# A normalised Gram matrix in the setup of a deformable-convolution kernel: norms applied to the images before, to the 64x64 products after

## What is computed

```python
x_flat = x.reshape(B, C, H * W)
nrm = jnp.linalg.norm(x_flat, axis=2, keepdims=True)
x_n = x_flat / jnp.maximum(nrm, 1e-12)
cos = jnp.einsum('bcn,bdn->cd', x_n, x_n) / B
_, idx = jax.lax.top_k(-jnp.abs(cos).T, k)          # k = 2
s = x.sum(axis=(2, 3)); sq = (x * x).sum(axis=(2, 3))
gs = s + s[:, idx[:, 1:]].sum(axis=-1)              # sums of the pair
...
x_hat = (x - mean[:, :, None, None]) * inv[:, :, None, None]
```

## Time and profile before

| | |
|---|---|
| median of 3 runs | 427.45 us (426.53 to 428.62) |
| the profiled execution, its own time | 429.34 us |
| its span, first to last instruction | 427.5 us |
| TensorE busy | 398.2 us, 93% |
| ScalarE busy | 327.0 us, 76% |
| VectorE busy | 312.3 us, 73% |
| GpSimd busy | 111.4 us, 26% |
| copy to `neg_cos` starts | 22.61 us |
| TensorE starts on the first layer | 27.97 us |

### The profile page before, as it was taken

The page is one execution under the profiler, slowest core; times in us unless marked ns, Lnnn a source line. Parts: engine busy times, 40 slices in busy tenths (PEclk is TensorE's granted clock), DMA queues, the critical chain, the costliest instruction groups (busy, mean ns, idle before and its releaser), DMA issues.

```text
span 427.5 us, 19117 instructions
## 1 busy us (share of the span) xinstructions
PE 398.2 (93%) x7747; PEld 357.9 (84%) x7747; DVE 312.3 (73%) x868; ACT 327.0 (76%) x423; POOL 111.4 (26%) x241
## 2 busy tenths in 40 slices
PE   4978899999999999999998899999999998999980
PEld 4865689999999999999885788999999997998870
DVE  3649877788887777777438888877777776777445
ACT  2617788888888898888835878888888887888745
POOL 6303223222222222238001322232222222220000
PEclk9999999999999999999999999999999999999996
DMA  6301342211122222222001231222222222222005
GB/s 220 84 2 34 71 69 48 45 36 36 38 46 46 44 44 46 49 48 41 2 3 28 57 62 38 50 45 46 45 45 45 48 48 47 48 48 40 3 2 196
DMA packets 61529, 21.28 MB, mean 50 GB/s; under 512 B 53798, under 2 KB 61308, under 8 KB 61484
## 3 DMA queue, kind: packets, MB, share of 16 engines
q1 hardware_dynamic: 56588, 18.20, 20.3%
q0 software_dynamic: 4896, 2.43, 2.2%
HBM read 3.23 MB, written 2.10 MB: 12 GB/s over the span
## 4 chain that ended last, share of the span: by engine, by line
PE 85%; DVE 5%; DMA 4%; ACT 2%; issue 2%; SPq 1%; POOL 1%; DVEq 0%; ACTq 0%; POOLq 0%
PE acc_ps L746 54%; PE z_ps L719 12%; PE build_ps L704 8%; PE side_ps L652 3%; PE acc_ps L770 3%; PE side_ps L641 2%; DMA xs<-in_x 2%; PE build_ps L588 1%; DMA moved<-conv_sb 1%; PE acc_ps L598 1%; DMA feat_rows<-feats 1%; ACT raw L563 1%; PE acc_ps L630 1%; SPq L278 1%; ACT S L482 0%
## 5 line engine op out<-in xcount | busy, mean ns | idle before, releaser
L746 PE MATMUL acc_ps<-S,Z 64*64 64x256 f32 x4416 | 279.4, 377 | 1.6 <-issue 0.9
L746 PEld LDWEIGHTS acc_ps<-S,Z 64*64 64x64 f32 x4416 | 225.3, 133 | 19.8 <-issue 3.5
L482 ACT ACTIVATE S<-build_ps,minus 128x1024 f32<-128x1024 f32 x190 | 201.5, 1112 | 30.6 <-PE build_ps L704 30.2
L719 PE MATMUL z_ps<-wz,xflat 64*64 64x192 f32 x1536 | 106.9, 328 | 0.0
L704 PE MATMUL build_ps<-feat_rows,cst 64*64 64x512 f16 x576 | 82.9, 377 | 3.3 <-ACT S L482 1.6
L475 ACT ACTIVATE Z<-z_ps 128x768 f32<-128x768 f32 x96 | 78.2, 814 | 4.9 <-PE z_ps L719 4.9
L719 PEld LDWEIGHTS z_ps<-wz,xflat 64*64 64x64 f32 x1536 | 75.8, 132 | 6.5 <-issue 1.3
L1007 DVE TENSOR_SCALAR S<-build_ps 128x512 f32<-128x512 f32 x96 | 66.1, 688 | 19.1 <-PE build_ps L704 17.3
L278 POOL DMA_DIRECT2D moved<-conv_sb x140 | 71.0, 514 | 20.6 <-POOL conv_sb L371 15.5
L1009 DVE TENSOR_SCALAR S<-build_ps 128x512 f32<-128x512 f32 x96 | 65.3, 680 | 0.0
L371 POOL TENSOR_TENSOR conv_sb<-conv_sb,cst 128x32 f32<-128x32 f32 x28 | 7.5, 269 | 200.5 <-ACT conv_sb L469 200.5
(11 more groups left out here) (116 smaller groups left out, 307.4 us busy)
## 6 DMA issues: line engine op xcount, KB each, us to landing
xs<-in_x SPq DMA_DIRECT2D x4, 512.0 KB, 7.5
out<-raw SPq DMA_DIRECT2D x7, 256.0 KB, 2.5
moved<-conv_sb POOLq DMA_DIRECT2D x56, 11.2 KB
moved<-conv_sb SPq DMA_DIRECT2D x56, 11.2 KB
moved<-conv_sb POOLq DMA_DIRECT2D x56, 11.3 KB
wz<-in_dcn_w POOLq DMA_DIRECT2D x2, 288.0 KB, 4.7
feat_rows<-feats SPq DMA_TRANSPOSE x32, 3.7
moved<-conv_sb SPq DMA_DIRECT2D x28, 12.0 KB
```

Of the source, the lines that this page charges most:

```text
L482: act.activation(S[:, (parity + b) % 2, half, 0:ACT_TAPS, :], build_ps[:, 0:ACT_TAPS, :], ACT.Relu, bias=minus2[:, :], scale=1.0 if half = ...
L719: mm = pe.matmul(z_ps[halves[c], i, h * BLOCK_COLS:(h + 1) * BLOCK_COLS], xflat[parity][halves[i], pixels], wz[halves[i], layer, h, b * BL ...
L746: mm = pe.matmul(acc_ps[halves[i], g, 0:HW], Z[halves[g], slot, i, half, j * C:(j + 1) * C], S[halves[g], slot, half, j, :].rearrange(by_i ...
```

## The change

TensorE now turns the images as they were loaded, and each image's 64x64 Gram product is kept for itself. The norms come in afterwards: an entry (c, d) of an image's product is multiplied by the reciprocal norm of row c and that of column d. The row's is `rinv` as before, a number for each partition. The columns' is made on TensorE: a product of `rinv`, spread over 64 columns, with the identity over 32 (`spread_rinv`) puts each image's reciprocals in every row of a 64x64 tile in `z_ps`. VectorE multiplies all three (`scale_dots`), from a copy of the products that ScalarE makes (`keep_gram`). Then 16 products with `fold` sum the images and the two halves at once (`fold_dots`), in the place of the scaling and the one product before.

The work goes by chunks: TensorE's order is turn(g), spread_rinv(g-1), gram(g), fold_dots(g-1). The ten fill products ahead are gone; two stand behind gram(0). `fold` is no longer loaded but made on GpSimd from the identity, as is `ident_by_count`. The scalings of the images are gone, L870 and L430. Nothing behind the copy to `neg_cos` is changed.

```diff
-        xn = raw
-        xn_t = S[:, 0, 0, :, :]
+        x_t = [S[:, 0, j // 2, j % 2, :] for j in range(4)]
+        dots = raw[:, :, 0:C]
+        kept_gram = raw[:, :, C:2 * C]
...
+        turn_banks = ((build_ps[:, 0, :], build_ps[:, 1, :]), (build_ps[:, 2, :], z_ps[:, 0, :]))
...
+            pool.wait_ge(ident_in, 16)
+            pool.wait_ge(cleared, 8)
+            for rows in halves:
+                pool.tensor_scalar(ident_by_count[rows, :], ident[rows, rows], 1.0 / B, None, ALU.mult).then_inc(folds_made, 1)
+            pool.wait_ge(folds_made, 2)
+            for rows in halves:
+                pool.tensor_copy(fold[rows, :].rearrange("p (c n) -> p c n", c=2),
+                                 ident[rows, rows].unsqueeze(1).broadcast_to([C, 2, C])).then_inc(folds_made, 1)
...
+                act.wait_ge(x_turned, j + 1)
+                if j >= 4:
+                    act.wait_ge(gram_done, j // 2 - 1)
+                act.activation(x_t[j % 4], turn_banks[j // 2 % 2][j % 2], ACT.Copy).then_inc(x_t_ready, 1)
+
+            def keep_gram(g):
+                act.wait_ge(gram_done, g + 1)
+                act.activation(kept_gram[:, g * CHUNK_PAIRS:(g + 1) * CHUNK_PAIRS, :],
+                               acc_ps[:, g % 2, 0:CHUNK_PAIRS * C].rearrange("p (t c) -> p t c", c=C), ACT.Copy).then_inc(gram_kept, 1)
...
-            norm(0)
-            for g in range(X_CHUNKS - 1):
-                act.wait_ge(rinv_step, 2 * (g + 1))
-                for t in (g * CHUNK_PAIRS + 2, g * CHUNK_PAIRS + 3):
-                    act.activation(xn[:, t, :], xs[:, t, :], ACT.Copy, scale=rinv[:, t:t + 1]).then_inc(xn_by_act, 1)
-                norm(g + 1)
+            for g in range(X_CHUNKS):
                 copy_turned(2 * g)
                 copy_turned(2 * g + 1)
-            copy_turned(PAIRS // 2 - 2)
-            copy_turned(PAIRS // 2 - 1)
+                norm(g)
+                keep_gram(g)
...
-            keep_busy(10)
...
+            def turn(g):
+                pe.wait_ge(x_in[g], 16)
+                if g >= 2:
+                    pe.wait_ge(x_t_ready, 2 * (g - 1))
+                for j in range(2):
+                    for i in range(2):
+                        for h in range(HALVES):
+                            q = 2 * i + h
+                            mm = pe.transpose(turn_banks[g % 2][j][:, q * P:(q + 1) * P],
+                                              xs[:, CHUNK_PAIRS * g + 2 * j + i, h * P:(h + 1) * P], ident)
+                    mm.then_inc(x_turned, 1)
+
+            def gram(g):
+
+                if g >= 2:
+                    pe.wait_ge(gram_kept, g - 1)
+                for n in range(CHUNK_PAIRS):
+                    if n % 2 == 0:
+                        pe.wait_ge(x_t_ready, 2 * g + n // 2 + 1)
+                    for h in range(HALVES):
+                        for i in range(2):
+                            at = (n % 2 * HALVES + h) * P + i * C
+                            slab = x_t[(2 * g + n // 2) % 4][:, at:at + C]
+                            mm = pe.matmul(acc_ps[halves[i], g % 2, n * C:(n + 1) * C], slab, slab,
+                                           start=(h == 0), stop=(h == HALVES - 1))
+                mm.then_inc(gram_done, 1)
+
+            def spread_rinv(g):
+
+                pe.wait_ge(rinv_step, 2 * (g + 1))
+                if g == 0:
+                    pe.wait_ge(folds_made, 4)
                 else:
+                    pe.wait_ge(scaled_dots, CHUNK_PAIRS * g)
+                for n in range(CHUNK_PAIRS):
+                    t = CHUNK_PAIRS * g + n
                     for i in range(2):
+                        mm = pe.matmul(z_ps[halves[i], 1, n * C:(n + 1) * C], rinv[halves[i], t:t + 1].broadcast_to([C, C]),
+                                       ident_by_count[halves[i], :], start=True, stop=True)
+                mm.then_inc(rinv_rows, 1)
+
+            def fold_dots(g):
+                for n in range(CHUNK_PAIRS):
+                    t = CHUNK_PAIRS * g + n
+                    pe.wait_ge(scaled_dots, t + 1)
+                    mm = pe.matmul(side_ps[:, 0, 0:C], fold[:, :], dots[:, t, :], start=(t == 0), stop=(t == PAIRS - 1))
+                return mm
 
             turn(0)
-            for j in range(1, PAIRS // 2):
-                turn(j)
-                gram(j - 1)
-            gram(PAIRS // 2 - 1)
-            pe.wait_ge(setup_dve, 1)
-            pe.wait_ge(consts_in, 16)
-            pe.matmul(side_ps[:, 0, 0:C], fold, gram_sb[:, :], start=True, stop=True).then_inc(gram_step, 1)
+            gram(0)
+            keep_busy(2, side_ps[:, 1, 0:P])
+            for g in range(1, X_CHUNKS):
+                turn(g)
+                spread_rinv(g - 1)
+                gram(g)
+                fold_dots(g - 1)
+            spread_rinv(X_CHUNKS - 1)
+            fold_dots(X_CHUNKS - 1).then_inc(gram_step, 1)
...
+            def scale_dots(g, n):
+
+                t = CHUNK_PAIRS * g + n
+                if n == 0:
+                    dve.wait_ge(rinv_step, 2 * (g + 1))
+                    dve.wait_ge(gram_kept, g + 1)
+                    dve.wait_ge(rinv_rows, g + 1)
+                dve.scalar_tensor_tensor(out=dots[:, t, :], in0=kept_gram[:, t, :], scalar=rinv[:, t:t + 1],
+                                         in1=z_ps[:, 1, n * C:(n + 1) * C], op0=ALU.mult, op1=ALU.mult).then_inc(scaled_dots, 1)
...
-            dve.wait_ge(gram_step, PAIRS // 2)
-            dve.tensor_scalar(gram_sb[:, :], acc_ps[:, 0, 0:C], 1.0 / B, None, ALU.mult).then_inc(setup_dve, 1)
```

More of the change, by code:

```diff
@@ L569, in _, with keep_busy @@
             pe.wait_ge(ident_in, 16)
-            def keep_busy(count):
+            def keep_busy(count, into=build_ps[:, BLOCK_TAPS - 1, 0:P]):
                 for n in range(count):
-                    pe.matmul(build_ps[:, BLOCK_TAPS - 1, 0:P], ident, ident, start=True, stop=True, skip_group_check=True)
-            keep_busy(10)
-            def turn(j):
-                if j == PAIRS // 2 - 1:
-                    pe.wait_ge(xn_by_dve, 2 * (X_CHUNKS + 1))
-                else:
-                    pe.wait_ge(xn_by_act if j % 2 else xn_by_dve, 2 * (j // 2 + 1))
-                if j >= 2:
-                    pe.wait_ge(xn_t_ready, j - 1)
-                for i in range(2):
-                    for h in range(HALVES):
-                        q = 2 * i + h
-                        mm = pe.transpose(build_ps[:, j % 2, q * P:(q + 1) * P],
-                                          xn[:, 2 * j + i, h * P:(h + 1) * P], ident)
-                mm.then_inc(xn_turned, 1)
@@ L592, in gram @@
-            def gram(j):
-                pe.wait_ge(xn_t_ready, j + 1)
-                for q in range(4):
-                    for i in range(2):
-                        at = q * P + i * C
-                        slab = xn_t[:, j % 2, at:at + C]
-                        mm = pe.matmul(acc_ps[i * C:(i + 1) * C, 0, 0:C], slab, slab, start=(j == 0 and q == 0),
-                                       stop=(j == PAIRS // 2 - 1 and q == 3))
-                mm.then_inc(gram_step, 1)
-            turn(0)
@@ L603, in _ @@
-            for j in range(1, PAIRS // 2):
-                turn(j)
-                gram(j - 1)
-            gram(PAIRS // 2 - 1)
-            pe.wait_ge(setup_dve, 1)
-            pe.wait_ge(consts_in, 16)
-            pe.matmul(side_ps[:, 0, 0:C], fold, gram_sb[:, :], start=True, stop=True).then_inc(gram_step, 1)
+                    pe.matmul(into, ident, ident, start=True, stop=True, skip_group_check=True)
+            def turn(g):
[9 more added lines that the diff above has]
+                    mm.then_inc(x_turned, 1)
@@ L847, in _ @@
                 pe.wait_ge(bn_dve, BN_OPS * layer + 1)
-                pe.matmul(side_ps[:, 1, 0:2], fold, bmv[:, :], start=True, stop=True).then_inc(bn_folded, 1)
+                pe.matmul(side_ps[:, 1, 0:2], fold[:, :], bmv[:, :], start=True, stop=True).then_inc(bn_folded, 1)
                 if layer == 0:
@@ L1126, in shape_constants @@
     put("ident", np.eye(P))
-    put("fold", part[:, None] % C == part[None, :] % C)
     taps = np.arange(TAPS).reshape(BLOCKS, BLOCK_TAPS, 1)
```

76 lines of the change are left out of this document (40 added, 36 removed).

## The result

The changed kernel takes 432.49 us (median of 6 runs, 430.88 to 433.48), the kernel before 427.73 in its 6 runs: a ratio of 1.0112, 95% interval 1.0091 to 1.0133. Slower by 4.8 us, where 0.3 less was forecast.

A forecast was written before the change was run, and what follows sets the result against it. TensorE was taken to bound the setup, the layers staying unchanged. The steps put the neg_cos copy at 22.3 instead of 22.6 us, so -0.3 us and a median of 427.1, range 425.0 to 429.3 us.

The forecast's parts named there:

- The diff changes no instruction of that stretch: The two deformable layers, 28 to 415 us: 387 us long and unchanged, so only their start could move.
- a layer stretch that is not 387 us long: Sign of a wrong forecast: the two deformable layers, expected as long as before, take another time.
- nobody waits for: Setup: the ten fill products from 4.73 us in the kernel before, taken as work no engine needs.
- the start 5.8 us earlier: Setup: TensorE's real work begins at 4.73 instead of 10.51 us, no longer waiting for normalised images.
- -0.3: Forecast change in us: neg_cos copied at 22.3 instead of 22.6, everything behind it equal.
- Step 4 of the chain: Setup's end: last reciprocal rows to 21.1, four scalings to 21.8, last fold to 22.3, where neg_cos is copied.
- Step 1, the start: Chunk 0 at the low clock: x lands at 4.54, identity at 4.73; turns, copy, Gram and fill passes end at 9.3.
- near balance: Setup: some 5.6 us of added TensorE work over four chunks against a start 5.8 us earlier; called the forecast's core.
- no handover stalls in the middle: Setup chunks: a rival had TensorE wait 0.3 to 0.5 us a chunk, sum +0.6 to +1.2; chance 0.13.
- the second table load: ScalarE, 7.45 to 8.75 us: 1.28 us load before the root, its reciprocals by 9.6 wanted only at 10.85.
- The late rise: Rival, setup: clock rises late, +1.4 us at 14.0, +2.4 at 15.9, +5 or more if never; chance 0.15.
- Narrow folds: Rival, setup: folds at 0.04 us a pass and clock rise at 8.2 give -3.2 us; chance 0.17.

The follow-up runs named there:

- experiment 5: The kernel before, ten fills kept, plus 39 idle tiny TensorE products (156 instructions) ahead of the wait for the identity: 429.8 us, ratio 1.0058 to the kernel before.
- 6: The changed kernel plus 98 idle TensorE instructions, making 256 more than the kernel before: 430.67 us, ratio 1.0062 to the kernel before.
- experiment 7: The changed kernel with a root of a constant first on ScalarE, so the root's table is loaded first: 431.35 us, ratio 1.008 to the kernel before.
- experiment 9: The changed kernel with each fold as two products behind 64-column weights, instructions filled up to 256 more than before: 428.78 us, ratio 1.0028 to the kernel before.
- 10: Experiment 9 with VectorE's sums ahead of scalings, last reciprocal rows earlier in their own bank, root's table first: 428.15 us, ratio 1.001 to the kernel before.
- experiment 11: The reordered narrow-fold kernel with eight tiny 128x1 clears first on VectorE: 427.61 us, ratio 0.9989 to the kernel before.
- 4: The changed kernel with ten instead of six fill products behind the last folds: 431.74 us, ratio 1.0078 to the kernel before.
- experiment 8: The kernel before without its ten fills, ten tiny early products in their place: 428.8 us, ratio 1.002 to the kernel before.
- 1: The changed kernel once more, unchanged, for a second profile: profiled execution 433.08 us.
- 2: The kernel before once more, unchanged, for a second profile: profiled execution 428.34 us.

## Why the prediction was wrong

1. **"The diff changes no instruction of that stretch. So the question is only how early it may begin."** This step failed first. The layers have the same instructions, but each now stands 158 places later in TensorE's program. Where a block of 16 KB ends moves with that. In before both block changes fall under a wait of TensorE for something else, in after under dense products, and cost 1.79 and 1.61 us, of which about 1.4 reached the layers' length. Experiment 5 shows that idle instructions alone bring both stalls into the kernel before, and 6 that filling up to 256 takes both away. In the profiles that is worth 1.3 us beside the fall of the clock (401.9 to 399.7 us, 0.9 of it the fall). The ratios say from 0.002 (against experiment 7 beside it) to 0.005 (against the first runs of after). That a late block is what stops TensorE is read from this and from the packet ahead of each stall; why these two take 2.5 us to be of use, while most others stop nothing, is open, and the bursts of transfers around them are a rival that no run tests. The Trainium skill, Runtime: NRT & Kernel Launch, section Instruction fetch mechanics, has the engine fetch its program in blocks of 16 KB, 256 instructions, and calls the cost of crossing mostly hidden. The block size agrees with the packets, 0.54 MB in 33; two crossings of after were not hidden. The low-clock stretches add to it in single executions, in both kernels. The prediction had named "a layer stretch that is not 387 us long" as a sign of being wrong, and that came: from TensorE's start on the first layer to the end it is 401.9 us for 399.6.

2. **The baseline.** The sum was made against an execution whose clock rose at 14.0, and took that as the kernel's own, though at 429.34 us it lay above all six timed runs (426.53 to 428.62). Such a time is rare but not unheard of for this kernel: of its timed executions up to 431 us in the later experiments, four are longer. Its second profile and experiment 5 show rises at 9.0 and 8.3 inside the fill products, which I had called work that "nobody waits for". They can carry the rise: without them it is at 13.1 and behind weak ones at 17.9, each in one profile, but with them it was at 14.0 once as well. So the start 5.8 us earlier is not all gain: it puts real work at the low level into the time in which fills brought the clock up for the kernel before. Between like executions the chain is 2.1 us longer (18.0 to 18.2 against 15.75 to 16.1), where -0.3 stood.

3. **Step 4 of the chain, mis-sized.** The end from 21.4 took 2.8 us, forecast 1.9. Three terms: the scalings 0.19 apart instead of 0.15; "the last fold, 0.43", where after the first scaled product all four folds run, 1.12 us, since each takes 0.22 to 0.28 and none was done before; and 0.48 us of VectorE issue ahead of the copy. Experiments 9 and 10 took away cost of the folds and of the waits around them, 11 the issue.

4. **Step 1, the start**: the landing of x 0.37 later. It is 4.52 and 4.54 in the two profiles of before and 4.75 to 5.06 in the eleven others, also where the number of TensorE's instructions is that of before. What does it is open.

5. **The "near balance" of 5.6 us of added work against a start 5.8 us earlier** does not follow from the prediction's own prices: 3.5 less 2.4 is 1.1 us a chunk, 4.4 over four. The sum of -0.3 does not rest on it, as it was added up step by step. Along those steps `neg_cos` came 1.9 us late (24.21 for 22.3): 0.4 at the landings, 0.3 more by the end of the first chunk's folds (14.10 for 13.4), 0.3 in chunks 2 and 3, and 0.9 at the end.

What held: a chunk takes 3.6 us (3.5 forecast) and TensorE is its bound; a fold pass behind 128 columns takes 0.11 us and the reciprocal rows 0.61; the rise, 11.08 for 10.5, with 8.2 to 11.1 over the profiles of the changed setup; no handover stalls in the middle; the second table load is hidden. On this the Trainium skill, ScalarE: Activation LUTs, section What ACT_TABLE_LOAD costs, has a drain of 1380 ns beside the load; ScalarE's timeline of after shows the next function 0.01 us behind it:

```profile
7.73 1.28 ACT L444 ACT_TABLE_LOAD   x1
9.02 0.20 ACT L444 ACTIVATE rinv<-sums 128x4 f32<-128x4 f32 x1
```

The late rise, the rival on the slower side, had the sign right and the cause wrong: the clock rose in time. "Narrow folds" was no property of 64 columns but of the weights, and had to be written (experiment 9).

By size, of the median's 4.8 us: about 2.1 is the longer chain, 0.4 the landing, 1.4 the instruction stalls. The remaining 0.9 may be low-clock stretches that come more often; how often they come in either kernel is not known from two profiles each, and stays open. Nor is the 4.8 itself known to a microsecond: experiments 4 and 7, which keep both stalls, have 1.0078 and 1.008, some 3.4 us.

## What to carry to other kernels

When TensorE's instructions change in number, look at "issue" pieces in the chain of the untouched part, and pad up to a multiple of 256 with idle products to see what the work itself costs. Take two profiles of the kernel before, if the clock's rise is in what you count. Early work that feeds nobody may be what brings the clock up, though experiment 8 shows no clear loss without it; replacing it with useful work at the low level may gain less than the earlier start.

## What was not expected of the hardware

- 156 instructions in an idle stretch cost 0.27 to 0.88% of the time (experiment 5), and one of the stalls comes 235 us behind them, at 240.41.
- VectorE has such a gap too, 0.47 to 0.48 us ahead of `neg_cos` in after and in experiments 1, 4, 6, 7, 9 and 10, where that is its 64th instruction; eight more ahead removed it there (experiment 11). That it is the same thing is argued, not shown.
- The clock's rise varies between executions of one kernel, 9.0 and 14.0 in before, 8.8 and 11.1 in after. It also falls to 0.51 for 3.4 us of busy TensorE work, at 28, 46, 231 or 244 us, in both kernels, and in some executions not at all. Each of the seven falls comes close behind idle time of TensorE. In experiments 1, 4 and 5 that is one of the instruction stalls: they end at 243.24, 242.68 and 45.46, and the clock falls at 244.31, 243.72 and 45.85. In after and experiment 7 it is the waits at the setup's end, in experiments 2 and 8 those at the second layer's start. None of the four profiles filled up to 256 has a fall. So the stalls may cost a low stretch on top of themselves; that is argued, not shown.
- A float32 product of 64 columns is spaced 0.11 us a pass behind weights of 128 columns and 0.04 in side-by-side pairs behind weights of 64.
